# Moving a row normalization from VectorE to GpSimd in a GNN + LSTM kernel

## The reference

```python
# first layer
h = relu(adj @ (x @ Wg0 + bg0));  h = relu(adj @ (h @ Wg1 + bg1))
for p in 1, 2, 3, 4:                      # windows of p neighbouring nodes
    wins = h in windows of p nodes
    h[last node of each window] = last hidden state of an LSTM (weights p) over its window
x1 = layernorm(x + h)                      # (v - mean) / sqrt(var + eps), over the features
# second layer
A_hat = symmetric normalization of adj + I
h = relu(batchnorm((A_hat @ x1) @ W1.T + b1))
out = layernorm(x1 + batchnorm(h @ W2.T + b2))
```

## Time and profile before

| | us |
|---|---|
| median of 3 runs | 808.98 |
| lowest, highest | 808.69, 810.32 |
| the profiled execution | 809.28 |
| its span in the trace | 807.5 |
| busy in the span: PE | 777.1 (96%) |
| busy: DVE | 720.0 (89%) |
| busy: ACT | 592.3 (73%) |
| busy: POOL | 114.9 (14%) |
| chain that ended last: PE / DVE / ACT | 79% / 10% / 5% |

### The profile page before, as it was taken

One profiled execution on the slowest core, in us unless ns is written; L12 is line 12 of the kernel. 1 busy time (PEld: TensorE's weight loads), 2 busy tenths in 40 slices (PEclk: granted clock), 3 DMA queues, 4 the chain that ended last, 5 costly groups with the idle time before them and its releaser, 6 DMA issues.

```text
span 807.5 us, 15612 instructions
## 1 busy us (share of the span) xinstructions
PE 777.1 (96%) x4976; PEld 532.0 (66%) x4976; DVE 720.0 (89%) x1834; ACT 592.3 (73%) x1178; POOL 114.9 (14%) x125
## 2 busy tenths in 40 slices
PE   8999999999999999999999999999999988899985
PEld 5666777677767777777777777776766655344542
DVE  4787989999999999999999999999999989688996
ACT  4667777777777777777777777777867754895398
POOL 0000000000000000000000000000000001586695
PEclk9999999999999999999999999999999999999999
DMA  5010001010101010101010101010000000154245
GB/s 200 26 40 14 1 28 53 27 53 28 53 28 53 26 52 26 52 26 52 26 52 26 52 26 52 27 53 28 27 27 28 27 27 27 53 182 157 81 179 208
DMA packets 17549, 44.44 MB, mean 55 GB/s; under 512 B 2016, under 2 KB 3168, under 8 KB 17376
## 3 DMA queue, kind: packets, MB, share of 16 engines
q1 hardware_dynamic: 17504, 43.87, 15.1%
HBM read 27.09 MB, written 16.78 MB: 54 GB/s over the span
## 4 chain that ended last, share of the span: by engine, by line
PE 79%; DVE 10%; ACT 5%; issue 3%; DMA 1%; SPq 1%; POOL 1%; ACTq 0%; DVEq 0%; POOLq 0%
PE gate_bank L948 14%; PE gate_bank L949 14%; PE gate_bank L963 6%; PE gate_bank L973 6%; PE gate_bank L1020 4%; PE back_bank L902 3%; PE front_bank L858 3%; ACT z L1138 3%; PE front_bank L863 3%; PE front_bank L869 3%; PE front_bank L875 3%; PE gate_bank L932 3%; PE gate_bank L933 3%; PE gate_bank L934 3%; PE gate_bank L956 3%
## 5 line engine op out<-in xcount | busy, mean ns | idle before, releaser
L948 PE MATMUL gate_bank<-h_hi,w_hi 128*128 128x256 f16 (+2 forms) x528 | 162.7, 308 | 4.4 <-DVE h_lo L1351 2.9
L949 PE MATMUL gate_bank<-h_hi,w_lo 128*128 128x256 f16 (+2 forms) x528 | 162.5, 308 | 0.0
L1081 ACT ACTIVATE gate_i<-gate_bank,lstm_bias 128x512 f32<-128x512 f32 (+2 forms) x176 | 99.7, 567 | 62.6 <-PE gate_bank L973 32.0
L1081 ACT ACTIVATE gate_o<-gate_bank,lstm_bias 128x512 f32<-128x512 f32 (+2 forms) x176 | 100.2, 569 | 30.4 <-PE gate_bank L973 20.0
L963 PE MATMUL gate_bank<-h_lo,w_hi 128*128 128x256 f16 (+2 forms) x384 | 116.1, 302 | 0.0
L754 POOL TENSOR_TENSOR rstd<-veps,neg_half 128x8 f32<-128x8 f32 x15 | 26.3, 1753 | 630.4 <-DVE veps L1273 630.4
L948 PE MATMUL gate_bank<-s_hi,w_hi 128*128 128x256 f16 (+2 forms) x384 | 112.7, 302 | 0.6 <-DVE s_hi L1348 0.4
L949 PE MATMUL gate_bank<-s_hi,w_lo 128*128 128x256 f16 (+2 forms) x384 | 112.6, 301 | 0.0
L1334 DVE SCALAR_TENSOR_TENSOR gate_f<-gate_o,gate_f 128x512 f32<-128x512 f32 (+2 forms) x176 | 94.7, 538 | 19.2 <-ACT gate_f L1087 18.2
L1087 ACT ACTIVATE gate_f<-cell 128x512 f32<-128x512 f32 (+2 forms) x176 | 89.7, 510 | 28.5 <-DVE cell L1331 14.7
L1081 ACT ACTIVATE gate_g<-gate_bank,lstm_bias 128x512 f32<-128x512 f32 (+2 forms) x176 | 99.6, 566 | 0.7 <-PE gate_bank L956 0.2
(11 more groups left out here) (261 smaller groups left out, 1730.0 us busy)
## 6 DMA issues: line engine op xcount, KB each, us to landing
x_front<-in_x SPq DMA_DIRECT2D x16, 512.0 KB, 4.1
x_kept<-normed_sb SPq DMA_DIRECT2D x16, 512.0 KB, 2.6
z<-x_kept SPq DMA_DIRECT2D x16, 512.0 KB, 3.7
rows_sb<-in_x SPq DMA_DIRECT2D x15, 512.0 KB, 3.3
out<-z SPq DMA_DIRECT2D x15, 512.0 KB, 3.1
z<-in_wr SPq DMA_DIRECT2D x1, 1536.0 KB, 7.2
out<-z SPq DMA_DIRECT2D x2, 256.0 KB, 2.6
z<-in_wih SPq DMA_DIRECT2D x1, 192.0 KB, 2.4
```

The lines of the kernel that those rows point to most:

```text
L948: mm(dst, w[0], v[0], start=start, stop=False)
L949: mm(dst, w[1], v[0], start=False, stop=False)
L1081: ins = activation(acts[gate][h][:, 0:n], gate_bank[h][bank_of(job, gate)][:, 0:n], ACT.Tanh if gate == "g" else ACT.Sigmoid, bias=lstm_bi ...
```

## The change

In the planned part, that is for halves 0 to 14, the two `normed` steps go from VectorE to GpSimd, and stand there behind the power `rstd` of the same half. The eight `tensor_scalar` instructions of a half are the same as before, with the same operands. GpSimd takes over the wait for the previous store of `normed_sb`; it waits for its own power through the semaphore `rstd`. TensorE and SyncE wait for the semaphore `normed` as before. GpSimd no longer uses `run` with its loop: all its steps are written out with constants, chunk by chunk. The planner is told that `normed` costs 1.3 us on POOL (before: 1.02 us on DVE) and gets signal delays from POOL to PE (0.2) and to POOL (0.1). The table `AHEAD_OP` (111 entries before) is replaced as a whole, so that the order of PE, ACT and DVE work of all stages is another one. The back of half 15 keeps its normalization on VectorE.

```diff
     ops.append(("POOL", ("back", "rstd"), 1.62, [("back", "moments", 2)]))
     for n in range(2):
-        ops.append(("DVE", ("back", "normed", n), 1.02, [("back", "rstd")]))
+        ops.append(("POOL", ("back", "normed", n), 1.3, [("back", "rstd")]))
...
-             "DVE": {"PE": 0.18, "DVE": 0.13, "ACT": 0.13, "POOL": 0.16}, "POOL": {"DVE": 0.2}}
+             "DVE": {"PE": 0.18, "DVE": 0.13, "ACT": 0.13, "POOL": 0.16}, "POOL": {"DVE": 0.2, "PE": 0.2, "POOL": 0.1}}
...
 AHEAD_OP = {
...
-    ('DVE', 'back', ('back', 'normed', 1)): -0.3,
-    ('ACT', 'back', ('back', 'mixed', 0)): -1.7,
-    ('DVE', 'back', ('back', 'mixed_low', 0)): 1.85,
-    ('PE', 'back', ('back', 'mix', 1, 0)): -0.95,
...
+    ('DVE', 'back', ('back', 'moments', 1)): 1.85,
+    ('DVE', 'back', ('back', 'moments', 2)): 0.15,
+    ('PE', 'back', ('back', 'mix', 0, 0)): -0.9,
+    ('PE', 'back', ('back', 'mix', 1, 0)): -1.1,
...
+        def normalize(eng, src, dst, comb_t, rstd_t, n):
+            for b in range(4 * n, 4 * n + 4):
+                at = slice(b * P, (b + 1) * P)
+                last = eng.tensor_scalar(flat(dst[:])[:, at], flat(src[:])[:, at], comb_t[:, 2, b:b + 1],
+                                         rstd_t[:, b:b + 1], ALU.subtract, ALU.mult)
+            return last
...
             def emit(op, g, h):
-                wait(pool, ("back", "moments", 2), g, h)
-                signal(nc.gpsimd.tensor_tensor(rstd[0][:], veps[0][:], neg_half[:], ALU.pow), op, h)
-
-            run(pool, "POOL", emit)
+                if op == ("back", "rstd"):
+                    wait(pool, ("back", "moments", 2), g, h)
+                    ins = nc.gpsimd.tensor_tensor(rstd[0][:], veps[0][:], neg_half[:], ALU.pow)
+                else:
+                    n = op[2]
+                    if n == 0:
+                        wait(pool, ("back", "rstd"), g, h)
+                        if 2 * g + h > 0:
+                            pool.wait_ge(sem_kept, 16 * (2 * g + h))
+                    ins = normalize(nc.gpsimd, rows, normed, comb[0], rstd[0], n)
+                signal(ins, op, h)
+
+            for k in range(len(CHUNK_OF["POOL"])):
+                for q, op in CHUNK_OF["POOL"][LOOP_FROM if LOOP_FROM <= k < LOOP_TO else k]:
+                    emit(op, k + q // 2, q % 2)
...
-                elif what == "normed":
-                    if n == 0:
-                        wait(dve, ("back", "rstd"), g, h)
...
-                    ins = normalize(rows, normed, comb[0], rstd[0], n)
...
-                normalize(rows, normed, comb[0], rstd[0], n).then_inc(last_normed, 1)
+                normalize(ve, rows, normed, comb[0], rstd[0], n).then_inc(last_normed, 1)
```

More of the change, by code:

```diff
@@ L331 @@
[L331 to L339 removed]
+    ('PE', 'front', ('mix0', 'product', 0, 0)): -1.4,
+    ('PE', 'front', ('mix0', 'product', 1, 0)): -1.05,
@@ new lines @@
+    ('ACT', 'front', ('mix0', 'out', 1)): -1.9,
+    ('PE', 'front', ('lin0', 'product', 0, 0)): -1.3,
+    ('DVE', 'front', ('lin0', 'biased', 0)): -0.35,
+    ('ACT', 'front', ('lin0', 'out', 0)): -0.3,
+    ('PE', 'front', ('lin0', 'product', 1, 0)): -0.85,
+    ('ACT', 'front', ('lin0', 'out', 1)): -0.65,
+    ('PE', 'front', ('lin1', 'product', 0, 0)): -0.15,
+    ('DVE', 'front', ('lin1', 'out', 0)): -0.15,
+    ('PE', 'front', ('lin1', 'product', 1, 0)): -0.6,
+    ('PE', 'front', ('mix1', 'product', 0, 1)): -0.65,
@@ new lines @@
+    ('ACT', 'front', ('mix1', 'out', 0)): -0.6,
+    ('DVE', 'front', ('mix1', 'low', 0)): -0.9,
+    ('PE', 'front', ('mix1', 'product', 1, 0)): -0.35,
+    ('DVE', 'front', ('mix1', 'low', 1)): -0.9,
+    ('DVE', 'even', (('lstm', 1, 0), 'high')): 0.95,
+    ('DVE', 'even', (('lstm', 1, 0), 'low')): 1.35,
+    ('DVE', 'even', (('lstm', 1, 1), 'new')): 2.0,
+    ('DVE', 'even', (('lstm', 1, 1), 'high')): -0.1,
+    ('PE', 'even', (('lstm', 2, 0), 'gate', 'i')): -0.35,
+    ('PE', 'even', (('lstm', 2, 0), 'gate', 'g')): -0.7,
@@ new lines @@
+    ('DVE', 'even', (('lstm', 2, 0), 'new')): -1.4,
+    ('ACT', 'even', (('lstm', 2, 0), 'tanh')): -0.75,
+    ('DVE', 'even', (('lstm', 2, 0), 'hidden')): -0.95,
+    ('DVE', 'even', (('lstm', 2, 0), 'high')): -0.3,
+    ('PE', 'even', (('lstm', 2, 1), 'high', 'i')): -0.2,
+    ('PE', 'even', (('lstm', 2, 1), 'gate', 'f')): -0.95,
+    ('PE', 'even', (('lstm', 2, 1), 'input', 'o')): -1.05,
+    ('PE', 'even', (('lstm', 3, 0), 'gate', 'o')): -0.6,
+    ('PE', 'even', (('lstm', 3, 1), 'input', 'g')): -1.1,
@@ new lines @@
+    ('PE', 'even', (('lstm', 3, 1), 'high', 'g')): -0.25,
+    ('PE', 'even', (('lstm', 3, 1), 'input', 'o')): -0.55,
+    ('DVE', 'even', (('lstm', 3, 1), 'new')): -0.3,
+    ('DVE', 'even', (('lstm', 3, 1), 'hidden')): -0.45,
+    ('DVE', 'even', (('lstm', 3, 1), 'low')): 1.85,
+    ('PE', 'even', (('lstm', 3, 2), 'input', 'i')): -0.55,
+    ('PE', 'even', (('lstm', 3, 2), 'high', 'i')): -0.15,
+    ('PE', 'even', (('lstm', 3, 2), 'input', 'o')): -1.35,
+    ('ACT', 'even', (('lstm', 3, 2), 'act', 'i')): -1.6,
@@ new lines @@
+    ('DVE', 'odd', (('lstm', 1, 0), 'new')): 0.4,
+    ('DVE', 'odd', (('lstm', 1, 0), 'hidden')): -0.4,
+    ('PE', 'odd', (('lstm', 1, 1), 'gate', 'i')): -0.2,
+    ('PE', 'odd', (('lstm', 1, 1), 'gate', 'o')): -0.95,
+    ('DVE', 'odd', (('lstm', 1, 1), 'hidden')): 0.3,
+    ('PE', 'odd', (('lstm', 2, 0), 'gate', 'i')): -0.6,
+    ('ACT', 'odd', (('lstm', 2, 0), 'act', 'i')): -1.6,
+    ('ACT', 'odd', (('lstm', 2, 0), 'tanh')): -1.15,
+    ('PE', 'odd', (('lstm', 2, 1), 'input', 'g')): -1.95,
@@ new lines @@
+    ('PE', 'odd', (('lstm', 3, 1), 'high', 'i')): -1.25,
+    ('PE', 'odd', (('lstm', 3, 1), 'input', 'o')): -1.15,
+    ('ACT', 'odd', (('lstm', 3, 1), 'act', 'g')): -0.8,
+    ('DVE', 'odd', (('lstm', 3, 1), 'cell')): 1.55,
+    ('DVE', 'odd', (('lstm', 3, 1), 'low')): 1.6,
+    ('PE', 'odd', (('lstm', 3, 2), 'input', 'i')): -0.9,
+    ('PE', 'odd', (('lstm', 3, 2), 'high', 'i')): -1.45,
+    ('DVE', 'odd', (('lstm', 3, 2), 'new')): -0.7,
+    ('DVE', 'odd', (('lstm', 3, 2), 'hidden')): -0.85,
@@ new lines @@
+    ('ACT', 'odd', (('lstm', 4, 2), 'act', 'i')): -0.3,
+    ('DVE', 'odd', (('lstm', 4, 2), 'high')): -0.55,
+    ('PE', 'odd', (('lstm', 4, 3), 'input', 'i')): -1.3,
+    ('PE', 'odd', (('lstm', 4, 3), 'input', 'o')): -0.5,
+    ('ACT', 'odd', (('lstm', 4, 3), 'tanh')): 1.1,
+    ('DVE', 'back', ('back', 'residual', 0)): 0.25,
+    ('DVE', 'back', ('back', 'stats', 0)): -0.65,
+    ('DVE', 'back', ('back', 'stats', 1)): 0.3,
+    ('DVE', 'back', ('back', 'moments', 0)): -0.1,
+    ('DVE', 'back', ('back', 'moments', 1)): 1.85,
@@ L1274, in row_moments @@
                                                op1=ALU.add)
-            def normalize(src, dst, comb_t, rstd_t, n):
-                for b in range(4 * n, 4 * n + 4):
-                    at = slice(b * P, (b + 1) * P)
-                    last = ve.tensor_scalar(flat(dst[:])[:, at], flat(src[:])[:, at], comb_t[:, 2, b:b + 1],
-                                            rstd_t[:, b:b + 1], ALU.subtract, ALU.mult)
-                return last
             def back_rows(op, g, h):
```

152 lines of the change are left out of this document (42 added, 110 removed).

## The result

The changed kernel takes 859.94 us (median of 4 runs, 859.09 to 861.72) where the kernel before, in the same session, takes 809.65 (4 runs, 808.69 to 810.65): a ratio of 1.062, 95% interval 1.0605 to 1.064. I had forecast 806.3 us, with a range up to 812.0.

What follows compares the result with a forecast made beforehand. TensorE (PE) was taken to set the pace in the middle, with at most 1.2 us a turn to win. Terms -3.0 - 0.7 - 0.5 + 1.5 = -2.7 gave 806.6 us profiled, 806.3 as median; range 803.0 to 812.0.

Steps and rivals of the forecast that it cites:

- Their cost on POOL: The moved normed instructions on GpSimd: 0.34 us each, 1.3 for four, from a line between two traced operations.
- Contention: GpSimd and VectorE colliding on SBUF: VectorE pays 0.10 us per instruction, GpSimd two collisions of 0.22 in normed 0.
- Term 4: TensorE waiting at mix 0 for a late normed 0: +0.1 us in each of 15 halves, +1.5; ends 0 and +24.
- `mix` 1 is no issue: Second mix of a half: it waits for mixed_low 0 anyway, a chain longer than normed 1, so no cost.
- Terms 1 to 3: VectorE's relief and new order: -3.0 us from 98 to 590, -0.7 between 620 and 640, -0.5 between 650 and 670.
- The first rival: Middle turns: PE bound, the 1.2 us of holes have other owners, nothing to win; 809.0 us, chance 0.18.
- The second rival: VectorE's relief given back: POOL holds the port for whole instructions, VectorE pays 0.34 each; 810.0 us, chance 0.13.
- The third rival: Slower: mix 0 heads PE's queue and waits for GpSimd, 0.65 us a half, +9.8; 814.6 us, chance 0.22.
- Term 5: Free: POOL's time, GpSimd's wait for the normed_sb store, SyncE's store and POOL's written-out program cost nothing.
- Term 6: Half 15's back and the second layer, at the kernel's end, are unchanged: 0.

Runs made afterwards that it cites:

- The probe: The kernel before, with 32 tensor_scalar instructions added on GpSimd in its idle stretch, four of each of eight forms; 810.78 us beside 809.08.

## Why the prediction was wrong, step by step

The runs side by side. "Alone" is what the instructions of one `normed` would take on POOL undisturbed, count by shortest length.

```
order  pair             alone   time     turn    mix 0 late by, two halves
old    (add, mult)      0.9 us  810.14   82.52   0      0      (2 of 4 blocks)
old    (add, mult)      1.8     819.63   83.74   0.74   0.28
old    (subtract, mult) 3.2     842.02   86.31   1.96   1.61
new    (add, mult)      0.45    809.92   82.61   0      0      (1 of 4 blocks)
new    (add, mult)      0.9     813.23   82.99   0.09   0.18   (2 of 4 blocks)
new    (mult, add)      1.8     826.81   84.39   0.27   1.30
new    (subtract, mult) 3.2     859.94   88.85   1.30   2.62
```

"Late by" is power-to-`mix` 0 of that run less the room of its order: 324.52 - 318.08 = 6.44 less 3.82 is 2.62. It accounts for the turns. With the cheap pair in the new order 0.27 + 1.30 = 1.57 of the 84.39 - 82.61 = 1.78; in the old order 1.02 of the 1.22. With the dear pair in the old order, in a turn without a dip, 3.57 of the 86.31 - 82.52 = 3.79. After: 3.92 of the 88.85 - 82.61 = 6.24; 1.1 to 1.7 for the dip and 0.4 in front of `mix` 1 (below) bring it to 5.4 to 6.0, and the last 0.2 to 0.8 stay open.

**The step that failed: "Their cost on POOL".** I took 0.34 for one instruction and 1.3 for four, with ends of 0.8 and 3.1. It is 0.79 alone, 3.16 for four, beyond the upper end before anything is in its way. The line was drawn between a `tensor_tensor` product of 8 columns and a (mult, add) of 512; a (subtract, mult) of 512 columns costs 2.08, so neither end bounded it. A slope of columns was trusted where the trace showed no row of this pair. **"Contention"** was low too: I took two meetings of 0.22 in `normed` 0, 0.4 us. It was 0.7 and 1.0, inside my end of four at 0.37, but one instruction alone lost 0.79.

**Term 4, +1.5, had the place right and the size wrong.** I wrote that `normed` 0 would end 3.5 us after the start of the power; it ends 1.85 + 0.10 + 3.84 = 5.8 and 2.11 + 0.10 + 4.16 = 6.4 after it. The power itself is up to 0.36 longer than my 1.75. The rooms to `mix` 0 are 4.56 and 3.82, so with `normed` 0 at 3.5, as I had it, nothing would have waited: the cushion behind the planned 3.0 is 0.8 and 1.6, not my 0.4. It could have been read beforehand: the new plan's own times put `mix` 0 at 4.27 and 3.64 us after the start of the power. The two prices of POOL's time turned +1.5 into 34.5 us of standing TensorE, above the end of +24. On top came 14.8 us of lower clock, for which I had no term at all.

**"`mix` 1 is no issue"** holds in the old order, where `mix` 1 comes 4.8 to 5.7 us behind `mix` 0, and only nearly in the new one, where it comes 2.6 to 2.8 behind. In the half in which `mix` 0 waits 1.13, `mix` 1, whose matmuls follow 3.1 us later, waits 0.39 again: POOL needs 4 x 0.79 = 3.1 us for `normed` 1 even undisturbed. The old order carries the dear pair for 842.0, the new one for 859.9. Turn against turn that is 88.85 against 86.31, 2.5 us. The lateness of `mix` 0 is 0.35 of it (3.92 against 3.57), the wait of `mix` 1 another 0.4, the dip of the clock 1.1 to 1.8: between 98 and 600 us the new order has five, the old one has one. By the mean clocks, 0.979 and 0.993, the clock is 18.0 - 5.9 = 12.1 of the 19.4 us between the two spans, the larger part. The new order has the longer waits, 2.46 us against 1.6 to 2.0, but since equal waits stand with a dip and without one, their length does not settle it alone.

**Terms 1 to 3, -4.2, were nothing.** VectorE's busy time in a turn fell to 73.5 as forecast (about 73). With that relief and no late POOL the time is 810.14, with a third of it 809.57: not under the kernel before. So the 1.2 us a turn that I took as holes of TensorE, itself from a sum of rounded distances (its terms make 40.5 us a half, not 40.6; the 81.1 is right), are not won by relieving VectorE. What they are is open. The first rival had this right, and I gave it 0.18; its time, 809.0, was as wrong as mine. That VectorE is 93% busy in a turn misled me. Between 620 and 640 us, where I took 0.7, TensorE in the run with half of the blocks is busy 19.00 of 20 with VectorE at 17.84, against 19.01 and 19.52: the hole stays.

**The second rival, relief given back through the port,** is not borne out. The old-order runs with 120 and 64 of the instructions have 701.5 and 696.0 us of VectorE's busy time: 5.5 / 56 = 0.098 us for each POOL instruction. My 0.10 was right on VectorE's side. The Trainium skill's rule of a lock for the whole instruction ("SBUF — State Buffer", section "SBUF: two separate sides") would take more from VectorE, with instructions of 0.45 and more on POOL; the runs show 0.098. On POOL's side the trace goes part of the way with the rule: the instruction that begins at 320.29 loses 0.79 us. Blocked until the two VectorE operations that it meets end, at 321.29, it would have ended at 322.08; it ended at 321.87. The loser of these meetings is GpSimd, and I had priced that side too low. The probe shows the same loss: of four equal instructions (a subtraction alone) two take 1.57 and 1.34 us beside VectorE's two-input operations, and the two behind them 0.60. That it is the port, and not something else that the two engines share, no run here separates.

**The third rival** named the right place, head of TensorE's queue, but priced it from the same wrong cost of POOL, 1.3 us for four, so its 814.6 and its 0.22 were both too small. Term 5 was right for the written-out program (809.17) and for the store: POOL is idle for only 1.6 us in all in front of its new instructions. Term 6 stands: from the first power of half 15 to the end it is 126.1 us before and 125.7 after.
